# A mixture-of-experts stage whose routing weight moves from the input of "up" to the result of "down"

## The reference, cut to what matters

```
n = layernorm(x)                                # [2048, 128]
p = softmax(n @ router_w)                       # [2048, 8]
p = where(p is among the top 2 of its row, p, 0); p = p / sum(p)
for e in range(8):
    h = silu(n @ gate_proj[e]) * (n @ up_proj[e])   # [2048, 352]
    x += p[:, e] * (h @ down_proj[e])
```

## Time and profile before

| | |
|---|---|
| three runs | 2969.46, 2974.94 (median), 2979.68 us |
| profiled execution | 2967.82 us, span 2966.0 us |
| mean granted TensorE clock | 0.891 |
| PE, DVE, ACT, POOL busy | 2491.8, 2271.7, 1871.8, 890.7 us |
| last layer norm starts, routing starts | 2658.7 us, 2671.4 us |
| first and last expert matmul start | 2702.33 us, 2959.18 us |
| store of the output issued | 2961.75 us |

### The profile page before, as it was taken

The page is one execution under the profiler, slowest core; times in us unless marked ns, Lnnn a source line. Parts: engine busy times, 40 slices in busy tenths (PEclk is TensorE's granted clock), DMA queues, the critical chain, the costliest instruction groups (busy, mean ns, idle before and its releaser), DMA issues. The chain is left out here.

```text
span 2966.0 us, 35240 instructions
## 1 busy us (share of the span) xinstructions
PE 2491.8 (84%) x11867; PEld 1410.3 (48%) x11875; DVE 2271.7 (77%) x3096; ACT 1871.8 (63%) x2593; POOL 890.7 (30%) x494
## 2 busy tenths in 40 slices
PE   6689999998899999999999999995445666556998
PEld 3356666663344444444444444432235564444675
DVE  4487777773899999999999999984679995654443
ACT  4365555554799888899888888884345553123443
POOL 1021111111444444444344444440020002003665
PEclk8889999999899999999999999997566777557999
DMA  1000000001000000000000000000000101110000
GB/s 55 8 25 18 15 16 18 15 4 74 6 0 3 33 0 36 0 36 0 36 0 36 0 36 1 0 0 11 0 27 29 35 29 56 44 40 17 26 8 15
DMA packets 23168, 60.10 MB, mean 20 GB/s; under 512 B 2864, under 2 KB 14960, under 8 KB 21616
## 3 DMA queue, kind: packets, MB, share of 16 engines
q1 hardware_dynamic: 23024, 58.29, 5.7%
HBM read 53.04 MB, written 5.24 MB: 20 GB/s over the span
## 5 line engine op out<-in xcount | busy, mean ns | idle before, releaser
L251 PE MATMUL a_ps<-a_x,a_w 128*128 128x512 f32 x1536 | 695.6, 598 | 24.8 <-DVE a_kf L599 12.5
L251 PEld LDWEIGHTS a_ps<-a_x,a_w 128*128 128x128 f32 x1536 | 291.5, 191 | 404.4 <-issue 367.8
L774 POOL TENSOR_TENSOR a_den<-a_qf,a_ksum 128x1024 f32<-128x1024 f32 x128 | 271.2, 2119 | 510.3 <-DVE a_qf L592 473.7
L777 POOL TENSOR_TENSOR a_num<-a_qf,a_kvsum 128x1024 f32<-128x1024 f32 x128 | 295.0, 2304 | 186.1 <-DVE a_kvsum L617 185.9
L2281 DVE TENSOR_REDUCE x_rn<-x_sqk 128x8 f32<-128x512 f32 x256 | 174.3, 681 | 105.6 <-ACT x_sqk L2205 101.5
L2205 ACT ACTIVATE x_sqk<-x_b_k 128x512 f32<-128x512 f32 x256 | 153.1, 598 | 156.7 <-PE x_b_k L2117 150.2
L262 PE MATMUL a_ps<-a_att,a_w 128*128 128x512 f32 x480 | 215.8, 592 | 0.0
L2098 POOL TENSOR_TENSOR x_kn<-x_craw,x_w 128x256 f32<-128x256 f32 x64 | 47.0, 735 | 509.6 <-DVE x_craw L2270 488.1
L592 DVE SCALAR_TENSOR_TENSOR a_qf<-a_eq,a_qf 128x1024 f32<-128x1024 f32 x128 | 195.4, 1527 | 1.7
L445 ACT ACTIVATE a_den<-a_den,consts 128x1024 f32<-128x1024 f32 x128 | 147.0, 1149 | 55.3 <-POOL a_den L774 55.3
L599 DVE SCALAR_TENSOR_TENSOR a_kf<-a_ek,a_ps 128x1024 f32<-128x1024 f32 x128 | 155.5, 1215 | 27.9 <-ACT a_ps L441 23.4
(11 more groups left out here) (416 smaller groups left out, 5493.6 us busy)
## 6 DMA issues: line engine op xcount, KB each, us to landing
a_w<-layers SPq DMA_DIRECT2D x8, 2577.0 KB, 9.8
x_craw<-ctx SPq DMA_DIRECT2D x32, 256.0 KB, 2.7
y_cx<-ctx_t SPq DMA_DIRECT2D x16, 512.0 KB, 3.5
m_w<-experts SPq DMA_DIRECT2D x8, 608.0 KB, 3.9
x_w<-xattn_w SPq DMA_DIRECT2D x1, 2048.0 KB, 7.4
x_all<-x_t SPq DMA_DIRECT2D x1, 1024.0 KB, 4.9
t_scratch<-t_q_t SPq DMA_DIRECT2D x4, 256.0 KB, 3.7
t_scratch<-t_k_t SPq DMA_DIRECT2D x4, 256.0 KB, 5.5
```

Of the source, the lines that this page charges most:

```text
L251: last = nc.tensor.matmul(bank(tile, j), col(par, part * HK + u * P, P), x[:, t0:t0 + BANK], start=True, stop=True)
L774: nc.gpsimd.tensor_tensor(by_batch(den[:, b, :]), by_batch(qf[:, b, :]), bcast(ksum[:, b, :], S), ALU.mult).then_inc(d_ready, 1)
L777: nc.gpsimd.tensor_tensor(by_batch(num[:, b, :]), by_batch(qf[:, b, :]), bcast(kvsum[:, b, :], S), ALU.mult).then_inc(n_ready, 1)
```

## The change

The selecting matrix, the spread, `xw` and its split are gone. Gate and up both read `xn_hi` and `xn_lo`, split once in quarters. The routing weights `wt` are stored to a scratch tensor in DRAM, and SP fetches for every unit its half row broadcast over 128 partitions into `wb` (two buffers, by half). When down of a unit is ready, VectorE multiplies it by `wb` into `share` and adds `share` to x: two instructions in place of one. The fourth PSUM tile serves as a second tile for up; scores and transposes use `tile_o`. Routing has no block of its own: its scores come first on TensorE, its VectorE steps stand between the hidden products of unit 0, its transposes behind chunk 1 of unit 1. All loops are written out straight. Per unit TensorE has 54 matmuls in place of 58. A new expert's weights are split at the same place as before, at the end of an even unit.

```diff
-        tile_g, tile_u, tile_o, tile_w = banks = [...]
+        tile_g, tile_u0, tile_u1, tile_o = banks = [...]
+        tile_u = (tile_u0, tile_u1)
+        scratch = nc.dram_tensor("m_scratch", (EXPERTS, TOK), F32, kind="Internal").ap()
...
             @block.sync
-                with sp.Fori(0, (EXPERTS - 2) // 2) as pair:
...
+                def weights_of(k):
+                    wait_past(sp, weighed, k - 1)
+                    half = k % 2
+                    sp.dma_start(wb[:, half, :], scratch[k // 2:k // 2 + 1, half * HALF:(half + 1) * HALF].broadcast_to([P, HALF])
+                                 ).then_inc(wb_loaded[half], 16)
+                def expert(e):
+                    sp.wait_ge(w_lo_done, e - 1)
+                    sp.dma_start(w[:, e % 2, :], dram["experts"][e]).then_inc(e_loaded[e % 2], 16)
+                sp.wait_ge(w_kept, 2)
+                sp.dma_start(scratch, wt[:, :]).then_inc(w_stored, 16)
+                sp.wait_ge(w_stored, 16)
+                for k in range(2):
+                    weights_of(k)
+                for k in range(2, UNITS):
+                    if k % 2 == 0 and k // 2 + 1 < EXPERTS:
+                        expert(k // 2 + 1)
+                    weights_of(k)
             @block.tensor
-                def spread(k, par, half):
...
+                def gate_up(k, c):
+                    par, half = place(k)
+                    f0, fn = ECH[c]
+                    n = 3 * k + c
+                    if c == 0 and half == 0:
+                        pe.wait_ge(w_lo_done, k // 2 + 1)
+                    if c == 0 and k < 2:
+                        pe.wait_ge(xn_lo_done, 2 * k + 2)
+                    wait_past(pe, silu_done, n)
...
+                    wait_past(pe, hid_done, n - 1)
...
                 def down(k):
                     pe.wait_ge(hid_lo_done, 3 * k + 3)
-                    wait_ahead(pe, added, k)
+                    if k == 0:
+                        pe.wait_ge(w_kept, 2)
+                    wait_past(pe, weighed, k)
...
+                route()
+                for c in range(3):
+                    gate_up(0, c)
+                gate_up(1, 0)
+                gate_up(1, 1)
+                turn(0)
+                turn(1)
+                gate_up(1, 2)
+                down(0)
+                for k in range(2, UNITS):
+                    gate_up(k, 0)
+                    gate_up(k, 1)
+                    down(k - 1)
+                    gate_up(k, 2)
+                down(UNITS - 1)
             @block.scalar
+                split_tokens(0)
+                split_weights(0)
+                for p in range(1, 4):
+                    split_tokens(p)
+                act.wait_ge(shifted, 1)
+                nc.scalar.activation(prob[:, :, :], prob[:, :, :], ACT.Exp).then_inc(exped, 1)
+                for k in range(UNITS):
+                    for c in range(3):
+                        silu(k, c)
+                        if 3 * k + c:
+                            hid_high(3 * k + c - 1)
+                        if k == 1 and c == 1:
+                            keep(0)
+                            keep(1)
+                    if k == 0:
+                        split_weights(1)
+                    elif k % 2 == 0 and k // 2 + 1 < EXPERTS:
+                        split_weights(k // 2 + 1)
+                hid_high(3 * UNITS - 1)
             @block.gpsimd
...
             @block.vector
+                def output(k):
+                    half = k % 2
+                    dve.wait_ge(down_done, k + 1)
+                    dve.wait_ge(wb_loaded[half], 16 * (k // 2 + 1))
+                    wait_past(dve, added, k)
+                    nc.vector.tensor_tensor(share[:, :], tile_o[:, :], wb[:, half, :], ALU.mult).then_inc(weighed, 1)
+                    dve.wait_ge(weighed, k + 1)
+                    nc.vector.tensor_tensor(x_in[:, t], x_in[:, t], share[:, :], ALU.add).then_inc(added, 1)
+                split_tokens(0)
+                split_weights(0)
+                split_tokens(1)
+                shift_scores()
+                split_tokens(2)
+                split_tokens(3)
+                rank_start()
+                dve.wait_ge(exped, 1)
+                steps.done(normalise())
+                rank_by(1)
+                hidden(0, 0)
+                for s in (2, 3, 4):
+                    rank_by(s)
+                hidden(0, 1)
+                for s in (5, 6, 7):
+                    rank_by(s)
+                choose()
+                normalise().then_inc(weights_set, 1)
+                hidden(0, 2)
+                split_weights(1)
+                for c in range(3):
+                    hidden(1, c)
+                output(0)
+                for k in range(2, UNITS):
+                    hidden(k, 0)
+                    hidden(k, 1)
+                    output(k - 1)
+                    hidden(k, 2)
+                    if k % 2 == 0 and k // 2 + 1 < EXPERTS:
+                        split_weights(k // 2 + 1)
+                output(UNITS - 1)
```

More of the change, by code:

```diff
@@ L1064, in l1_moe @@
[L1064 to L1108, removed]
@@ L1111, in bank @@
+        hid_hi_done, hid_lo_done = sem("hid_hi_done"), sem("hid_lo_done")
         def bank(ap, j):
             return ap[:, j * BANK:(j + 1) * BANK]
[L1114 to L1124, removed]
+        UNITS = 2 * EXPERTS
@@ L1126, in l1_moe, with place @@
+        def place(k):
+            return k // 2 % 2, k % 2
         with nc.Block() as block:
@@ L1156, in weights @@
                 def weights(par, c0, n, rows=P):
                     return w_hi[0:rows, par, c0:c0 + n], w_lo[0:rows, par, c0:c0 + n]
[L1159 to L1175, removed]
@@ L1177, in down, with route, turn @@
-                def down(k, par, half):
+                def route():
+                    pe.wait_ge(r_loaded, 16)
+                    for t in range(TILES):
+                        last = nc.tensor.matmul(tile_o[:, t * EXPERTS:(t + 1) * EXPERTS], xn[:, t * P:(t + 1) * P],
+                                                router[:, :], start=True, stop=True)
+                    last.then_inc(scores, 1)
+                def turn(i):
+                    if i == 0:
+                        pe.wait_ge(weights_set, 1)
+                    else:
+                        pe.wait_ge(w_kept, i)
+                    for t in range(TILES // 2):
+                        last = nc.tensor.transpose(tile_o[0:EXPERTS, t * P:(t + 1) * P], prob[:, i * (TILES // 2) + t, :], ident)
+                    last.then_inc(w_turned, 1)
@@ new lines, in gate_up @@
+                def gate_up(k, c):
[7 more added lines that the diff above has]
+                    wait_past(pe, silu_done, n)
+                    for j in range(2):
+                        last = product(bank(tile_g, j)[0:fn], weights(par, E_GATE + f0, fn), (xn_hi, xn_lo),
+                                       slice(half * HALF + j * BANK, half * HALF + (j + 1) * BANK))
+                    last.then_inc(g_ready, 1)
+                    wait_past(pe, hid_done, n - 1)
+                    for j in range(2):
+                        last = product(bank(tile_u[n % 2], j)[0:fn], weights(par, E_UP + f0, fn), (xn_hi, xn_lo),
+                                       slice(half * HALF + j * BANK, half * HALF + (j + 1) * BANK))
+                    last.then_inc(u_ready, 1)
@@ L1178, in down @@
+                def down(k):
+                    par, half = place(k)
                     pe.wait_ge(hid_lo_done, 3 * k + 3)
-                    wait_ahead(pe, added, k)
+                    if k == 0:
+                        pe.wait_ge(w_kept, 2)
+                    wait_past(pe, weighed, k)
                     for j in range(2):
@@ L1185, in down @@
                     last.then_inc(down_done, 1)
-                pe.sem_inc(down_done, 1)
-                pe.wait_ge(xn_lo_done, 2)
-                spread(0, 0, 0)
-                all_units(pe, unit, down)
+                route()
[12 more added lines that the diff above has]
+                    gate_up(k, 2)
@@ L1264, in unit @@
-                def unit(k, par, half, prev, first):
-                    for c, (f0, fn) in enumerate(ECH):
-                        dve.wait_ge(silu_done, 3 * k + (c + 1))
-                        dve.wait_ge(u_ready, 3 * k + (c + 1))
-                        nc.vector.tensor_tensor(hid[0:fn, half, c, :], tile_u[0:fn, :], sg[0:fn, (half + c) % 2, :],
-                                                ALU.mult).then_inc(hid_done, 1)
-                        if c == 1 and not first:
-                            down(k - 1, prev, 1 - half)
-                        if c == 0 and not (isinstance(k, int) and k == 2 * EXPERTS - 1):
-                            weigh(k + 1, 1 - half)
-                    if not half and not (isinstance(k, int) and k == 2 * EXPERTS - 2):
-                        split_weights(k + 2, 1 - par)
@@ L1286, in _, with split_tokens, split_weights @@
[L1286 to L1289 removed]
```

(8 more changed lines are left out.)

142 lines of the change are left out of this document (62 added, 80 removed).

## The result

The median went from 2972.2 to 2922.6 us (four runs each), a ratio of 0.9836 with a 95% interval of 0.9812 to 0.9860: 49.6 us less (the interval is 42 to 56 us), where 42.5 were forecast. The profiled execution is the slowest of its four (2930.86 us, span 2929.1), and the reason lies outside the change: its routing starts at 2684.18 us instead of 2671.43. So everything here is measured inside the stage, from the first router matmul on.

The account below looks back on a forecast made before the run. TensorE was taken to bound the experts' units, with routing leaving it waiting before them. Gains of 22.4 (start) and 21.3 (units) less 1.25 (output) gave 42.5 us: 2974.9 to 2932 us, range 2915 to 2953.

Parts of the forecast that it names:

- Start: 23.6 us earlier, 1.2 given back: Routing and first two units: first expert matmul 23.6 us earlier, third unit at 2711 instead of 2733.4, 22.4 us gained.
- The weight rows' way through memory: Routing weights stored and broadcast through DRAM: first row 7.0 us after the copy, later rows hidden, no cost.
- The hand-over is late next: 0.52 and 1.24 us: Last chunk's low part delays down: 8 waits of 0.52, 6 of 1.24 at new experts, with restarts 13.2 us.
- The turn-taking of VectorE and GpSimd: Two-input VectorE steps and GpSimd subtractions exclude each other; if merely slowed side by side, hand-over sum 2 us less.
- Output costs nothing inside, 1.25 us at the end: VectorE's weighted multiply and add after down: no cost inside the units, one more add of 1.25 us at the end.
- Waits for weights and the falls behind them, 8.2 and 10.7 us: Units from the third: removing six waits for low weights saves 8.2 us, the clock falls behind them 10.7 us.
- Clock in the units: three falls, 5.1 us: New waits before down at six experts: half bring a TensorE clock fall of 1.7 us, 5.1 us lost.
- Rival 2: Units: the clock falls at every down wait, 14 falls in place of 3, 18.7 us more, 2951 us; 12%.
- Rival 3: Start: VectorE late with every rank, both first units wait for it, 10 us more, 2942 us; 10%.
- 4 (instruction supply): Unrolled straight-line program starves TensorE of instructions: 7 to 14 stops, 15 to 31 us, 2955 us; 5%.
- 5 (the clock stays low): Units: clock does not come back after waits; at half the matmuls 75 us lost, 3008 us, slower than before; 3%.
- rival 1: Milder hand-over wait, clock stays up, routing not held up: 5.1 + 4.3 + 4 us better, 2919 us; 25%.

Follow-up runs that it names:

- down behind gate 2: Changed kernel with the previous unit's down product moved behind the gate product of chunk 2; median 2910.95 us, 0.980 of before.
- 128-row matmuls: Changed kernel plus a GpSimd copy lengthening each wait before down and four 128-row matmuls behind it; third unit to last up 212.20 us against 189.48.
- down by chunk: Changed kernel with down waiting per chunk, VectorE making the last unit's last two low parts, its output in halves; median 2902.45 us, 0.9767 of before.
- four matmuls back: Changed kernel with four 512-column matmuls put back between gate and up of chunk 1 from the third unit; third unit to last up 190.98 us against 189.48.

## Why the prediction was right, point by point

- *Start: 23.6 us earlier, 1.2 given back.* Right in the sum and in most of its steps. The waits for the hidden product and for the copy are the ones named, the 1.3 us for a silu is not. GpSimd held up two rank steps, as counted, but for 4.3 us in the profile, where the upper bound was 3.2. The clock fall at these waits, 2.4 us in the forecast, did not come in the changed kernel's own profile; it came in all seven other runs with this start (down behind gate 2 to the 128-row matmuls, and down by chunk), for 6.8 us each time, some 2.9 us lost. Those seven took 37.8 to 38.9 us, a gain of 23 to 24, where 22.4 were forecast. The profile's 35.6, a gain of 26.3, is in part luck: the clock stayed up, and the router products took 1.9 us less than before.
- *The weight rows' way through memory: 7.0 us from the copy, a microsecond or two late costs nothing.* 7.7 us measured. In this execution, whose down came early, it cost the first wait before down 0.68 us; later rows cost nothing.
- *Dense units: 175.0 us.* 174.44 measured once the waits were gone.
- *The hand-over is late next: 0.52 and 1.24 us.* 0.54 and 1.07 us. Waits and restarts come to 13.0 us (0.68 of them the first wait), forecast 13.2. Small lags at the other hand-overs, up to 0.08 us each and 2 us in all (189.5 - 174.4 - 13.0), were not in the sum. That the spread had covered it is shown by the four matmuls put back.
- *The turn-taking of VectorE and GpSimd* shows again at the split, and moving the subtractions behind the routing freed the rank steps. Both agree with the rule cited for it from the Trainium skill, "SBUF — State Buffer", section "Who interferes with whom": the split ends 1.15 us after the subtraction it met, where it lasts 1.29 us alone.
- *Output costs nothing inside, 1.25 us at the end.* Nothing inside even when doubled, and 1.26 us from the start of the last matmul to the end of the last add (1.65 before, 2.91 after). The tail as a whole is only 1.16 us longer, since the down product in it took 0.1 us less.
- *Waits for weights and the falls behind them, 8.2 and 10.7 us.* 18.9 us were counted together; 17.3 us came out when the wait alone was moved in the kernel before.
- *Clock in the units: three falls, 5.1 us.* Wrong. None came. I had taken the length of the wait for the cause; in the kernel before, the spread's 8-row matmuls stood right behind the wait, and the change removed them. Without them waits of up to 2.10 us between starts left the clock up, with them waits of 1.52 us did not. That the units beat the forecast by 3.8 us is this error of 5.1 us, less the small lags. Rival 2 (a fall at every down wait) falls with it, and so, in the units, does the warning cited there from the Trainium skill, "TensorE: Matmul & The Clock Gate", section "A second HAM failure mode: psum-queue depth-cycling": at idles of 0.4 to 1.7 us between full matmuls the clock never moved. In the start it is open. There the clock fell in one run behind starts 2.16 us apart (four matmuls back) and stayed up in another behind 2.19 us (changed). Rival 3 (VectorE late with every rank) would have put the third unit near 49.6 us behind the first router matmul; no run with this start took over 38.9. Rivals 4 (instruction supply) and 5 (the clock stays low) show nowhere: the clock in the units is 1.00, and idle with only the issue named is 1.8 us in the units.
- Of rival 1's three parts one came true in full, the clock in the units, and the others hardly.
- In the profiled execution the stage took 7.9 us less than its forecast: 4.0 in the start, which is mostly luck, 3.8 in the units, where the cause given for the clock was wrong, and 0.1 in the tail. The forecast of 42.5 us for the medians lies near the lower end of the measured interval of 42 to 56 us.

## What to carry to other kernels

When a stage's bounding engine loses work, look at what that work was covering: the next hand-over is due earlier by as much, and here it took back 15 us of 189, which a change of order by one product returned. A wait for several parts should be a wait for each part where it is used. Wait for what is read: one semaphore too strict had cost 17 us.

## What the runs showed of the hardware that I had not expected

- Behind the same waits, four matmuls of 512 columns with 8 rows went with a fall of the TensorE clock from 2.4 to 1.2 GHz in all of the units that have them (0.90 on average, 24.8 us), with 128 rows in none (1.00). In the units, starts 2.10 us apart with full matmuls on either side left it up. In the start of the stage it fell in six runs behind starts 2.83 to 2.87 us apart, also with full matmuls on either side.
- An instruction of VectorE that lasts 0.2 us alone lasted 2.40 us when it met a GpSimd subtraction, both reading two tensors from SBUF.
- The stages that were not touched differed by up to 19 us in their end from one execution to the next (2664.9 to 2684.2 us), more than most of the effects measured here: only stretches inside the stage could tell these apart.
